# z's matmul and reciprocal ahead of the memory product, output and residual behind it, in an attention loop over 32 sequences

## What is computed

```python
q, k, v = proj(Wq), proj(Wk), proj(Wv)          # x is 32 x 128 x 128
gate = sigmoid(betas)
def step(carry, qkv):                            # over the two segments
    mem, zc = carry
    sq = elu(qs) + 1.0
    mem = mem + einsum('bhsk,bhsv->bhkv', sq, vs)
    zc = zc + (elu(ks) + 1.0).sum(axis=-2, keepdims=True)
    scores = einsum('bhsk,bhtk->bhst', qs, ks) * scale
    att_dot = einsum('bhst,bhtv->bhsv', softmax(scores), vs)
    num = einsum('bhsk,bhkv->bhsv', sq, mem)
    den = sq.sum(axis=-1, keepdims=True) * zc
    att = gate * (num / den) + (1.0 - gate) * att_dot
    out_seg = att.reshape(Bx, L, H * DV) @ Wo
x = layernorm(x + attention(x))                  # then retention, then experts
```

## Time and profile before

| | us |
|---|---|
| median of 3 runs | 1077.17 (1076.81 to 1077.95) |
| the profiled execution | 1074.45 |
| its span, first to last instruction | 1072.6 |
| TensorE busy | 793.4 |
| VectorE busy | 635.9 |
| ScalarE busy | 571.7 |
| GpSimd busy | 510.3 |
| mean granted clock of TensorE | 0.876 |

### The profile page before, as it was taken

One profiled execution on the slowest core, in us unless ns is written; L12 is line 12 of the kernel. 1 busy time (PEld: TensorE's weight loads), 2 busy tenths in 40 slices (PEclk: granted clock), 3 DMA queues, 4 the chain that ended last, 5 costly groups with the idle time before them and its releaser, 6 DMA issues. The chain is left out here.

```text
span 1072.6 us, 26942 instructions
## 1 busy us (share of the span) xinstructions
PE 793.4 (74%) x9437; PEld 669.7 (62%) x9438; DVE 635.9 (59%) x1281; ACT 571.7 (53%) x1183; POOL 510.3 (48%) x524
## 2 busy tenths in 40 slices
PE   5788878878888878878878878878589570069950
PEld 4566767767767767767766767767456470069940
DVE  5766665766665676565666665666368553024438
ACT  5566665566766566676566666565312120057740
POOL 3455555445555445465445455445334214726643
PEclk8899899988989999999999999998789855579985
DMA  6644344534344544344544344544113900140014
GB/s 201 177 101 119 98 132 110 130 98 117 98 127 113 127 104 117 99 127 114 125 104 117 99 108 132 126 105 106 39 31 119 184 1 25 52 111 30 32 58 121
DMA packets 112933, 110.86 MB, mean 103 GB/s; under 512 B 6400, under 2 KB 100896, under 8 KB 108816
## 3 DMA queue, kind: packets, MB, share of 16 engines
q1 hardware_dynamic: 110368, 105.39, 38.4%
q0 software_dynamic: 2544, 5.21, 1.5%
HBM read 67.42 MB, written 43.16 MB: 103 GB/s over the span
## 5 line engine op out<-in xcount | busy, mean ns | idle before, releaser
L318 POOL TENSOR_TENSOR ps<-s_exp,row_rec 128x512 f32<-128x512 f32 x64 | 65.5, 1044 | 279.2 <-DVE row_rec L708 279.2
L300 POOL TENSOR_TENSOR lhs<-pos_qv,ungate 64x1024 f32<-64x1024 f32 x64 | 150.9, 2358 | 58.6 <-PE mix L343 56.1
L503 ACT ACTIVATE s_exp<-s_exp 128x512 f32<-128x512 f32 x64 | 40.3, 629 | 215.5 <-DVE s_exp L693 215.5
L638 DVE TENSOR_TENSOR lhs<-mix,zg_all 64x512 f32<-64x512 f32 x128 | 88.3, 690 | 81.4 <-PE mix L404 78.4
L362 PE MATMUL bank<-w_k,x_cur 128*128 128x512 f32 x192 | 72.1, 527 | 75.1 <-DVE z L698 71.5
L350 PE MATMUL bank<-w_o,attT 128*128 128x128 f32 x512 | 67.3, 286 | 52.9 <-ACT attT L512 52.9
L362 PEld LDWEIGHTS bank<-w_k,x_cur 128*128 128x128 f32 x192 | 44.0, 244 | 90.6 <-issue 82.2
L343 PEld LDWEIGHTS mix<-psT,lhs 128*64 128x64 f32 x2048 | 78.3, 161 | 33.8 <-issue 33.8
L350 PEld LDWEIGHTS bank<-w_o,attT 128*128 128x128 f32 x512 | 61.4, 196 | 59.9 <-issue 32.4
L531 ACT ACTIVATE e_qk<-bank 128x512 f32<-128x512 f32 x128 | 77.2, 603 | 28.8 <-PE bank L362 27.4
L343 PE MATMUL mix<-psT,lhs 128*64 128x64 f32 x2048 | 87.2, 249 | 5.6 <-issue 3.5
(11 more groups left out here) (209 smaller groups left out, 1723.3 us busy)
## 6 DMA issues: line engine op xcount, KB each, us to landing
scratch_qv<-qv_out SPq DMA_DIRECT2D x32, 1024.0 KB, 3.9
pos_qv<-scratch_qv SPq DMA_DIRECT2D x64, 512.0 KB, 6.6
zg_all<-scratch_z SPq DMA_DIRECT2D x64, 256.0 KB, 3.8
sorted_x<-padding SPq DMA_DIRECT2D x1, 2515.5 KB, 20.5
r_all<-in_x_dram SPq DMA_DIRECT2D x4, 512.0 KB, 6.0
cx<-in_ctx_dram SPq DMA_DIRECT2D x8, 256.0 KB, 2.8
w<-in_L_ffn_W_dram SPq DMA_DIRECT2D x1, 2048.0 KB, 9.7
y_tok<-y_rows SPq DMA_DIRECT2D x8, 256.0 KB, 4.9
```

What stands on the lines that cost most here:

```text
L300: pool.tensor_tensor(lhs[0:L, 1 - n, :, :], pos_qv[q][s, :, DK:], ungate[s, :, :], ALU.mult).then_inc(vg_ready, 1)
L638: dve.tensor_tensor(dst, mix[odd * DK:(odd + 1) * DK, g, :].rearrange("p (i n k) -> p i n k", n=SEG, i=4), zg_all[odd * DK:(odd + 1) * DK, ...
```

## The change

On TensorE output(t - 2) moves from ahead of turn_ps(0) to behind remember(1). z's matmul moves from behind the scores to between turn_ps(1) and remember(0). The second half of K's projection now also waits for the residual of three sequences back, since the output product and that projection share proj_bank 1 and the residual comes later. TensorE's first four steps are written out instead of two. On VectorE the reciprocal of z and its product with the gate move ahead of evac_memory, and the residual behind it. On GpSimd the four adds of k move ahead of the two products v times (1 - gate).

```diff
@@ GpSimd
+                if one:
+
+                    pool.wait_ge(sk_ready, 2 * t + 2)
+                    if not is_step(t, 0):
+                        pool.wait_ge(zc_ready, t)
+                    for i, c in enumerate((8, 4, 2, 1)):
+                        dst = e_qk[:, 0:c, DK:] if c > 1 else k_sum[:, :].unsqueeze(1)
+                        pool.tensor_tensor(dst, e_qk[:, 0:c, DK:], e_qk[:, c:2 * c, DK:], ALU.add).then_inc(k_summed, 1)
+                        pool.wait_ge(k_summed, 4 * t + i + 1)
+                if two:
                     if is_step(u, 0):
                         pool.wait_ge(gate_ready, 2)
...
-                if one:
-
-                    pool.wait_ge(sk_ready, 2 * t + 2)
...
+                if one:
                     for hh in range(2):
@@ TensorE
                     if not is_step(t, 0):
                         pe.wait_ge(v_evac, t)
+                    if not is_step(t, 0, 1, 2):
+                        pe.wait_ge(res_ready, t - 2)
                     project(proj_bank, w_k, 1, k_proj)
@@ TensorE
                     for f in range(4):
                         turn_qk(f)
+                if is_step(t, 0):
+                    pe.wait_ge(const_loaded, 16)
+                    pe.wait_ge(wo_loaded, 16)
+                if two:
+                    turn_ps(0)
+                    turn_ps(1)
+                if one:
+                    pe.wait_ge(k_summed, 4 * t + 4)
+                    pe.wait_ge(v_evac, t + 1)
+                    pe.matmul(proj_bank[0][0:SEG * H, 0:DK], cst("z_sum"), k_sum[:, :], start=True, stop=True).then_inc(zc_ready, 1)
+                if two:
+                    remember(0)
+                    remember(1)
                 if three:
...
                     output(t - 2)
-                if is_step(t, 0):
-                    pe.wait_ge(const_loaded, 16)
-                    pe.wait_ge(wo_loaded, 16)
-                if two:
-                    turn_ps(0)
-                    turn_ps(1)
-                    remember(0)
-                    remember(1)
                 if one:
                     score(0)
                     score(1)
-                if one:
-                    pe.wait_ge(k_summed, 4 * t + 4)
-                    pe.wait_ge(v_evac, t + 1)
-                    pe.matmul(proj_bank[0][0:SEG * H, 0:DK], cst("z_sum"), k_sum[:, :], start=True, stop=True).then_inc(zc_ready, 1)
                 if two:
                     turn_ps(2)
                     turn_ps(3)
 
-            run_steps(pe, step, B)
+            run_steps(pe, step, B, peeled=2)
@@ VectorE
-                if not is_step(t, 0, 1):
-                    residual(t - 2)
...
+                if one:
+                    dve.wait_ge(zc_ready, t + 1)
+                    if not is_step(t, 0):
+                        dve.wait_ge(z_ready, t)
+                    dve.reciprocal(z[:, :], proj_bank[0][0:SEG * H, 0:DK]).then_inc(z_rec, 1)
+                    dve.wait_ge(z_rec, t + 1)
+                    if not is_step(t, 0):
+                        dve.wait_ge(stored_z, 16 * t)
+                    dve.tensor_tensor(zg[:, :], z[:, :], gate[:, :], ALU.mult).then_inc(z_ready, 1)
                 if two:
                     evac_memory(0)
                     evac_memory(1)
                     evac_memory(2)
                     evac_memory(3)
+                if not is_step(t, 0, 1):
+                    residual(t - 2)
...
-                    dve.wait_ge(zc_ready, t + 1)
...
-                    dve.tensor_tensor(zg[:, :], z[:, :], gate[:, :], ALU.mult).then_inc(z_ready, 1)
```

## The result

The changed kernel takes 1125.78 us (1123.75 to 1129.32, four runs) against 1076.99 us: 1.0455 times the time before, 95% interval 1.0428 to 1.0483. It is slower by 49 us. The forecast was 1113 us with a range of 1098 to 1135, so sign and range held, and the 36 us of loss that it worked out were 13 too few.

The account below looks back on a forecast made before the run. Bound: a chain through all engines, none full. Per step 22.8 us at full clock plus 1.45 for a clock fall is 24.25 against 23.04; 30 steps add 36 us, giving 1113 us, forecast 1103 to 1121, range 1098 to 1135.

Parts of the forecast that it names:

- 22.8 us per step: Attention loop at full clock: distance of ScalarE's first K evacuations after the change, 0.56 above the 22.24 before.
- the residual's 0.73 us: VectorE, between last product and first maximum: residual's add and bn_stats delay maximum and shift by 0.73 us.
- The memory product started 12.3 us behind the first K evacuation: TensorE at full clock: memory product starts 12.3 us after ScalarE's first K evacuation; otherwise the sum is wrong.
- in time by 0.3 us: First scores, behind output on TensorE, readable near 305.4, 0.3 us before VectorE's maximum wants them at 305.7.
- z's matmul and GpSimd's order cost nothing: z's VectorE work fits idle time ahead of the products; both GpSimd orders are hidden, k's sum ready four microseconds early.
- The gap was to read 3.3 us: TensorE, from the q and k transposes to ps: 3.3 us without a matmul, lowering the clock in each step.
- a slow one behind an early z is harmless: K's projection: its first half is ready 1.5 us early, so a slow clock there, now costing 1.07 us, costs nothing.
- The price of a fall: Low clock behind the gap, at ps and memory product: 1.45 us per step, giving 24.25, between 23.9 and 24.5.
- rival B: Clock stays low twice as long, through memory product, output and scores: 24.7 to 25.5 us per step, 1127 to 1150; chance 0.13.
- Rival A: The clock stays up, or falls where harmless: 22.8 us per step, -7 us, 1070 us; chance 0.10.
- Rival C: The fall costs less than its half, as ScalarE and VectorE wait around it: step 23.0 to 23.8, 1077 to 1100; 0.09.
- Rival D: The residual does not reach the path: 22.2 us at full clock, 23.7 with the fall, 1097 us; chance 0.03.

Follow-up runs that it names:

- after_fill: The changed kernel plus twelve 128x512 matmuls, result unused, in TensorE's gap between the q and k transposes and ps: 1061.94 us, 0.9873 of before.
- res_behind: The changed kernel with twelve unused matmuls in the gap ahead of ps, and the residual moved behind the second shift: 1055.85 us, 0.9816 of before.
- out_behind_scores: The changed kernel with twelve unused matmuls in the gap, residual behind the second shift and output behind the scores: 1044.98 us, 0.9726 of before.
- z_only: The kernel before with only z's matmul, reciprocal and gate product moved ahead of the memory product, and GpSimd's new order: 1061.11 us, 0.9862 of before.
- pool_only: The kernel before with GpSimd's order alone changed, sum of k ahead of v times (1 - gate): 1075.55 us, 1.0004 of before.
- fill_turns: The changed kernel plus 24 float32 128x128 transposes of the identity, result unused, in the gap ahead of ps: 1062.38 us, 0.9887 of before.
- obs_no_fill: The changed kernel with output behind the scores and residual behind the second shift, without any fill in the gap: 1195.79 us, 1.1117 of before.
- before_fill: The kernel before plus eight unused 128x512 matmuls at each step's end, where TensorE waits for z: 1065.85 us, 0.9916 of before.
- small fill: The changed kernel plus one transpose and 80 unused 64x64 by 64-column products in the gap ahead of ps: 1350.58 us, 1.2598 of before.

## Why the prediction was right, and where its size was off

The bound was read rightly: a chain through all engines, closed by K's projection and by ScalarE's own queue. At full clock the forecast was 22.8 us per step, the output product 1.9 us ahead of the scores and the residual's 0.73 us on the path; after_fill measured 22.71. The memory product started 12.3 us behind the first K evacuation as forecast (298.39 against 286.00, 12.4). The scores were to be in time by 0.3 us: from the first product to the maximum it is 3.53 us in after_fill, 3.23 in res_behind and 2.88 in out_behind_scores (304.38 - 300.85, 301.69 - 298.46, 296.94 - 294.06), so they were 0.30 us early. The residual put 0.65 us on the path and not 0.73, since the maximum starts before bn_stats reads as ended. z's matmul and GpSimd's order cost nothing (z_only's 22.25 us at full clock, pool_only), and the wait on res_ready never shows in the changed kernel.

The gap was to read 3.3 us with qT at its end and reads 3.4 to 3.5; the fall was to come in every step, and there is no step of the steady part without one. That TensorE's idle time ahead of ps is the cause of these falls, and not the order, is shown by after_fill and fill_turns. K's projection is at full speed in every steady step of the changed kernel. That a slow one behind an early z is harmless, as forecast, z_only shows: the step that ends with one of 2.52 us takes 22.53 us, and the one with a fall in the same place and K at full speed 22.57.

The price of a fall was 1.45 us, the step 24.25 (23.9 to 24.5). 21 of 29 steps have a fall of this kind, and 24.11 us, a price of 1.40. In the step shown above it is made up of 0.87 us at ps, 0.12 at z's matmul and 0.54 at the memory product (distances of starts against after_fill), 1.53 for a step of 24.24.

The term that was mis-sized is rival B. The fall held three times as long in 8 of 29 steps, not twice as long, and made them 26.79 us: the memory product lost 1.65 us, output 1.7, and the slack of 0.3 ahead of the scores was used up, as its mechanism said. 0.89 at ps, 0.12 at z's matmul, 1.65 at the memory product, 0.80 of VectorE's waiting for output and 0.58 for the scores are 4.04 of the 4.08 us that such a step is above 22.71.

The prediction gave this case 0.13 as something that happens or doesn't, with a share of a third to all of the steps; it happened in 0.28 of them, and belonged into the forecast as a share. 8 x (26.79 - 24.11) / 29 = 0.74 us per step; 24.11 + 0.74 = 24.85 measured, against 24.25. Over 30 steps that is 18 us. The tail, which the sum put at nothing, gives 2.7 back, and the sum took 30 steps from 23.04 us where 29 distances from 23.08 are measured, which counts 2.8 too much. Of the 18 us 12.5 are left for the 13 between 1113 and 1126.

The earlier trace rows had shown a double fall, 6.7 us, in the kernel before; the row was read, and only priced as a rival. The sentence of the Trainium skill on transposes ("TensorE: Matmul & The Clock Gate", section "Part 4: PE-mode transpose") seemed to favour rival B; fill_turns, where transposes hold the high clock, gives it no support. Why the clock stayed low through a stretch in which TensorE was at work is not shown; idle time it was not.

Rival A (1070 us, the clock doesn't matter) is what after_fill makes true: 1062. Rival C (a fall costs less than its half, 23.0 to 23.8) holds in none of the 29 steps: the shortest is 23.95. Rival D, that the residual does not reach the path, does not hold either: moving it gains 0.27 us in res_behind, and 0.55 together with output.

## What to carry to other kernels

Work that stands in a wait may be holding the clock up. Before moving it, look at how long TensorE will be without work in that place, and what stands behind the gap: a fall that meets slack costs nothing (two steps of z_only), the same fall ahead of the chain cost 1.4 us here (24.11 against 22.71), and one that goes on cost 4. If the gap can't be closed, matmuls into a free bank whose result nobody reads are cheap. And a new order should be judged with the gap filled, or a good one (1045 us) looks like a bad one (1196 us).

## What the runs showed of the hardware

The clock had only its two levels, 1.00 and 0.50, in all runs. A fall behind a gap of 3.4 to 3.5 us held for some 3.3 us in most steps of the changed kernel, for 10.1 us and a little more in 8 of them, and for over 13.4 us in each step of obs_no_fill, the last with TensorE busy throughout, the 10.1 us with 9.69 of them busy: work without a break did not bring the clock back within that time. Most falls start in or behind a gap of 1.9 us or more, but not every such gap has one, and the fall of the earlier trace rows, 8 falls of before_fill and 3 of out_behind_scores start over 6 us behind TensorE's last idle time, in or behind the scores. At the low level the 64 matmuls of the memory product took 3.88 us instead of 2.23, the 16 of output 3.78 instead of 2.05, and 30 of the scores' 1.96 instead of 1.14. The small fill's instructions took 60 ns where those of the scores take 36 at the same clock; why is open.
